# A two-layer graph network on one core: subtracting the segment maxima on TensorE, and scanning in place in PSUM

## The chip, the cores and the metric

One core of one Trainium2 chip runs the whole program in one launch. Its engines are TensorE (PE, with its weight loads shown as PEld), VectorE (DVE), ScalarE (ACT), GpSimd (POOL) and SyncE (SP, which issues DMAs here). The metric is the device time of one execution in microseconds (us), as the median over several runs.

## The reference

6250 nodes of 128 features, 106,250 edges sorted by target node. Both layers gather a row of the source node for each edge, form a softmax over the edges that enter a node, and add up weighted rows per node:

```python
h = relu(layernorm(x))
# layer 0, softmax per feature
msg   = h[src] + edge_attr                      # [E, 128]
s     = msg * beta
m     = segment_max(s, dst)
e     = exp(s - m[dst])
denom = segment_sum(e, dst)
agg   = segment_sum(msg * (e / denom[dst]), dst)
x     = x + (agg @ H + bias + h)                # H from phm_rule and W
# layer 1: graph attention with 4 heads, one maximum per head, then elu
```

Only layer 0's `s - m[dst]` is touched by the change.

## The kernel before, in words

The edges are worked off in 208 groups (`NG`) of 512 (`GE`), each as four blocks of 128 edges on the partitions. Each engine has its own instruction stream, written as a software pipeline: `sweep_edges` runs a list of (lag, stage) pairs, so that in step s an engine does stage X of group s minus X's lag, in the order of the list. Semaphores tie the engines together. Nothing reorders the work: what is written first on an engine runs first.

Layer 0, for a group g, in the order of its data:

- SyncE loads the 512 edge rows into `msg` (ring of 8 groups), lists and flags for four groups at a time.
- GpSimd gathers the rows `h[src]` into `ring_h` with four indirect DMAs, 128 rows each (line 573, ring of 4 groups: `gather0(g)` waits for the lift of group g-4).
- ScalarE lifts `ring_h` into PSUM (`row_psum`, line 693), VectorE adds it to `msg` (`add0`, line 938).
- TensorE turns the messages, so that features lie on partitions and edges run along the columns, with four products by `beta_ident` (beta times the identity) into `bank[g % 2]` (`turn0`, line 1165).
- VectorE finds the segment maxima with two scans along the edges. A flag of minus 2^126 at each segment's start resets the running maximum. The first scan (line 917) runs forward over the turned messages into `run_max`; the second (line 920) runs backward over `run_max` and spreads each segment's maximum over its columns, into `seg_max`. A [128 x 1] instruction (line 927) computes by how much the maximum of a segment that is cut by the group's border has risen.
- VectorE subtracts: `diff` = turned messages minus `seg_max` (line 948). TensorE turns it back into `bank[2]` with four transposes (`unturn0`, line 1174).
- ScalarE exponentiates twice, into `wgt` (line 678, for the denominators) and into PSUM (line 681); VectorE multiplies the latter with `msg` (`products0`, line 955).
- TensorE adds up per node with one-hot matrices, eight f32 products of 128 columns (line 1156); ScalarE merges the sums into the accumulators in SBUF (lines 656 to 664).

The order of the stages in one step, with their lags: VectorE `add0` (0), `one_hot0` (0), `products0` (3), `maxima0` (1); TensorE `sums0` (4), `turn0` (0), `unturn0` (2); ScalarE `merge0` (5), `lift0` (0), `weigh0` (3); GpSimd `gather0` alone. A f32 product of 128 columns shows as two passes in the trace, a transpose as one.

Layer 1 uses the same `segment_max` on four partitions, one per head. There the first scan already writes to PSUM (`head_run`), and the second reads it from there.

Of the kernel before, what the change touches and what calls it, by code (L numbers as in the profile page):

```python
# [22 lines left out]
ALU = mybir.AluOpType  # L23
ACT = mybir.ActivationFunctionType

P = 128
# [33 lines left out]
def apart(eng):  # L60


    eng.nop(nofuse=True)


def later(item, n):

    return not isinstance(item, int) or item >= n


def gnn_kernel(nc, x_in, src_in, dst_in, ea_in, rule_in, w0_in, bias_in, beta_in, w1_in, a_in, out):
    N, D = x_in.shape
# [5 lines left out]
    GB = 4  # L78
    GE = GB * P
# [23 lines left out]
    with ctx:  # L103
        def sb(name, shape, dt=F32):
            return ctx.enter_context(nc.sbuf_tensor(name, shape, dt))
# [14 lines left out]
        ident = sb("ident", [P, P])  # L120
        beta_ident = sb("beta_ident", [P, P])
# [3 lines left out]
        head_mask = sb("head_mask", [P, H])  # L125
        head_spread = sb("head_spread", [H, D])
        head_pick = sb("head_pick", [P, H])
        junk = sb("junk", [1, 1])
        zero_row = sb("zero_row", [1, WIN], BF16)
        beta = sb("beta", [P, 1])  # L130
# [50 lines left out]
        msg = sb("msg", [P, RING, GB, TW])  # L181
        meta_g = sb("meta_g", [P, RING, 2 * GB], I32)
        flags = sb("flags", [P, 2, HALF * GE + 1], BF16)
        window = sb("window", [P, RING, GB, H])
        run_max = sb("run_max", [P, 2, GE])
        seg_max = sb("seg_max", [P, 2, GE])
        diff = sb("diff", [P, 2, GE])
        drop = sb("drop", [P, RING])
# [20 lines left out]
        head_run = sums[0:H, 1, 1, :]  # L209
        bank = [ctx.enter_context(nc.psum_tensor(f"bank{i}", [P, GE], F32)) for i in range(4)]  # L210
# [92 lines left out]
        L0, L1 = layer_sems(0), layer_sems(1)  # L303
# [468 lines left out]
        def _(dve):  # L772
# [74 lines left out]
            def h0(b, u, use):  # L847
                if u in DVE_SLOTS:
                    dve.wait_ge(ln0_numbers, b + 1)
                    if later(b, WXB):  # L850
                        dve.wait_ge(h_stored[u], 16 * use)
                    made = use * len(DVE_SLOTS) + DVE_SLOTS.index(u)
                    if later(b, 2):
                        dve.wait_ge(ln0_part, 3 * made)
                    apart(dve)
                    for t in range(GB):
                        ins = dve.tensor_scalar(run_max[:, 0, t * D:(t + 1) * D],
                                                nodes[:, bass.ds(b * GB + t, 1), :].rearrange("p a d -> p (a d)"),
                                                norm_b[:, u, 0, t:t + 1], norm_b[:, u, 1, t:t + 1], ALU.mult, ALU.add)
                    ins.then_inc(ln0_part, 1)  # L860
                    dve.wait_ge(ln0_part, 3 * made + 1)
                    lnx = run_max[:, 0, :].rearrange("p (t d) -> p t d", d=D)
                    dve.tensor_scalar(wgt[:, u, :, :], lnx, 0.0, None, ALU.max).then_inc(ln0_h[u], 1)
                    tiles = nodes[:, bass.ds(b * GB, GB), :]
                    dve.scalar_tensor_tensor(tiles, lnx, 0.0, tiles, ALU.max, ALU.add).then_inc(ln0_part, 2)

            sweep(dve, NBAT, WXB, [(0, h0)])


# [13 lines left out]
                    link(dve.tensor_tensor(phm[:, :, :], phm[:, :, :], phm_term[:, :, :], ALU.add))  # L883
            dve.sem_inc(phm_ready, 1)

            dve.tensor_scalar(beta_ident[:, :], ident[:, :], beta[:, 0:1], None, ALU.mult).then_inc(beta_ready, 1)

            for j in range(2):
                ins = dve.tensor_scalar(a_heads[:, j * H:(j + 1) * H], head_mask[:, :], a_col[:, j:j + 1], None, ALU.mult)
# [14 lines left out]

            def segment_max(g, s, use, k, n, data):
                par = s % 2
                run = run_max[0:n, par, :] if k is L0 else head_run
                run_end = run_max[0:n, 1 - par, GE - 1:GE] if k is L0 else seg_max[0:n, 1 - par, GE - 1:GE]
                lo = s % HALF * GE
                flag = flags[0:n, s // HALF, lo:lo + GE + 1]  # L910
                dve.wait_ge(k["flagged"][s // HALF], 16 * (use + 1))
                if isinstance(g, int) and g == 0:
                    before = -BIG
                else:
                    dve.wait_ge(k["dropped"], g)
                    before = run_end
                dve.tensor_tensor_scan(run, flag[:, 0:GE], data, before, ALU.add, ALU.max  # L917
                                       ).then_inc(k["scanned"], 1)
                dve.wait_ge(k["scanned"], 2 * g + 1)
                dve.tensor_tensor_scan(seg_max[0:n, par, ::-1], flag[:, GE:0:-1], run[:, ::-1], -BIG,  # L920
                                       ALU.add, ALU.max).then_inc(k["scanned"], 1)
                dve.wait_ge(k["scanned"], 2 * g + 2)
                if not (isinstance(g, int) and g == 0):
                    if later(g, RING):
                        dve.wait_ge(k["factored"], g - (RING - 1))

                    dve.scalar_tensor_tensor(drop[0:n, s:s + 1], run_end, seg_max[0:n, par, 0:1],
                                             flag[:, 0:1], ALU.subtract, ALU.add).then_inc(k["dropped"], 1)
                else:
                    dve.memset(drop[0:n, s:s + 1], 0.0).then_inc(k["dropped"], 1)  # L930
# [9 lines left out]
                                  ).then_inc(L0["added"], 1)  # L940

            def maxima0(g, s, use):
                par = s % 2
                dve.wait_ge(L0["msgT"], g + 1)
                segment_max(g, s, use, L0, P, bank[par][:, :])
                if later(g, 2):
                    dve.wait_ge(L0["unturned"], g - 1)
                dve.tensor_tensor(diff[:, par, :], bank[par][:, :], seg_max[:, par, :], ALU.subtract
                                  ).then_inc(L0["shifted"], 1)

            def products0(g, s, use):
                if later(g, 2):
# [102 lines left out]
            def maxima1(g, s, use):  # L1055
                dve.wait_ge(L1["msgT"], g + 1)
                segment_max(g, s, use, L1, H, bank[1][0:H, :])
# [60 lines left out]
        def _(pe):  # L1118
# [20 lines left out]
            for par in range(1):  # L1139
                for j in range(2):  # L1140
                    ins = pe.matmul(sums[:, par, j, :], zero_row[0:1, 0:P], zero_row[0:1, :], start=True, stop=True)
# [18 lines left out]
            def turn0(g, s, use):  # L1160
                pe.wait_ge(L0["added"], g + 1)
                if later(g, 2):
                    pe.wait_ge(L0["shifted"], g - 1)
                for b in range(GB):
                    ins = pe.matmul(bank[s % 2][:, b * P:(b + 1) * P], msg[:, s, b, 0:D], beta_ident[:, :],  # L1165
                                    start=True, stop=True)
                ins.then_inc(L0["msgT"], 1)

            def unturn0(g, s, use):
                pe.wait_ge(L0["shifted"], g + 1)  # L1170
                if later(g, 1):
                    pe.wait_ge(L0["weighed"], g)
                for b in range(GB):
                    ins = pe.transpose(bank[2][:, b * P:(b + 1) * P], diff[:, s % 2, b * P:(b + 1) * P], ident[:, :])
                ins.then_inc(L0["unturned"], 1)

            def sums0(g, s, use):
# [134 lines left out]
```

## Time and profile before

| | |
|---|---|
| median of three runs | 2367.47 us (2364.91 to 2371.19) |
| the profiled execution | 2366.12 us, span 2364.4 us |
| TensorE busy | 1784.6 us (75%) |
| VectorE busy | 2110.9 us (89%) |
| ScalarE busy | 1390.4 us (59%) |
| GpSimd busy | 1641.5 us (69%) |
| gathers of layer 0, first and last start | 67.8 and 1130.3 us |
| gathers of layer 1, first and last start | 1251.5 and 2294.7 us |

How to read it: the span is what the profiler saw between the first and the last instruction of one execution; the execution's own time is 1.7 us more, and lies 1.4 us under the median. Layer 0's edges take the time from about 68 to 1155 us, layer 1's from about 1251 to 2330. Busy shares are averages over both layers and the parts between them, so what bounds one layer has to be read inside it. An engine's "issue" idle time is time in which it waited for nothing that the profile shows.

### The profile page before, as it was taken

The page shows a single profiled execution, that of the slowest core. Times are in us where ns is not written, and L with a number is a line of the kernel's source. Part 1 is how long each engine was busy: PE and PEld are TensorE (multiplying, and loading weights), DVE is VectorE, ACT ScalarE, POOL GpSimd, SP SyncE. Part 2 cuts the span into 40 slices and gives each one's busy share as a digit, 9 for nine tenths or more (in the row PEclk, how much of TensorE's full clock was granted, in tenths as well). Part 3 has the DMA queues.
Part 4 walks back from the last instruction along what each step waited for, and adds up shares of the span by engine and source line. Part 5 has one row for each costly group of instructions (what it writes and reads, how often), then busy time and mean ns, then how long its engine had stood idle before and what let it go on. Part 6 is the DMA issues. An engine that isn't in the chain of part 4 may idle for free.

```text
span 2364.4 us, 61321 instructions
## 1 busy us (share of the span) xinstructions
PE 1784.6 (75%) x14154; PEld 1649.2 (70%) x14155; DVE 2110.9 (89%) x4087; ACT 1390.4 (59%) x3516; POOL 1641.5 (69%) x1735
## 2 busy tenths in 40 slices
PE   0466666666666666666557999999999999999986
PEld 0366666666666666666457888888888888888886
DVE  5799999999999999999666898888888888988885
ACT  2366666666666666666783555555555555555554
POOL 3677777777777777777216777777777777777761
PEclk9999999999999999999767999999999999999995
DMA  5544444444444444444013333333333333333321
GB/s 126 144 129 133 128 131 129 126 128 127 132 128 132 128 132 130 126 126 122 9 33 74 61 59 59 59 59 59 59 59 59 59 59 59 59 59 59 59 52 55
DMA packets 338883, 214.19 MB, mean 91 GB/s; under 512 B 170833, under 2 KB 305340, under 8 KB 338829
## 3 DMA queue, kind: packets, MB, share of 16 engines
q0 software_dynamic: 53248, 112.57, 20.1%
q1 hardware_dynamic: 285580, 101.01, 16.8%
q8 instruction: 22, 0.36, 0.1%
q14 instruction: 33, 0.26, 0.0%
HBM read 201.38 MB, written 10.30 MB: 90 GB/s over the span
## 4 chain that ended last, share of the span: by engine, by line
POOL 56%; issue 24%; DMA 7%; DVE 6%; PE 2%; ACT 2%; SPq 1%; POOLq 1%; DVEq 0%; ACTq 0%
POOL ring_h L573 28%; POOL msg L595 28%; DMA ring_h<-h_dram,meta_g 4%; DMA msg<-wx_dram,meta_g 2%; DVE sums L917 1%; DVE seg_max L920 1%; PE sums L1156 1%; DVE onehot L901 1%; DVE prod L1071 1%; POOL diff L584 1%; ACT sums L693 1%; ACT acc L664 0%; PE bank L1281 0%; PE bank L1224 0%; SPq L331 0%
## 5 line engine op out<-in xcount | busy, mean ns | idle before, releaser
L595 POOL DMA_INDIRECT msg<-wx_dram,meta_g x832 | 790.8, 950 | 293.5 <-issue 247.0
L573 POOL DMA_INDIRECT ring_h<-h_dram,meta_g x832 | 810.2, 974 | 259.9 <-issue 257.8
L1156 PE MATMUL sums<-onehot,prod 128*128 128x128 f32 x3328 | 696.2, 293 | 28.7 <-ACT acc L664 14.6
L1156 PE MATMUL sums<-onehot,wgt 128*128 128x128 f32 x3328 | 676.3, 287 | 0.0
L1156 PEld LDWEIGHTS sums<-onehot,prod 128*128 128x128 f32 x3328 | 536.7, 203 | 74.6 <-issue 71.6
L1156 PEld LDWEIGHTS sums<-onehot,wgt 128*128 128x128 f32 x3328 | 538.3, 204 | 0.0
L1165 PE MATMUL bank<-beta_ident,msg 128*128 128x128 f32 x1664 | 243.5, 290 | 347.3 <-DVE msg L938 347.3
L1165 PEld LDWEIGHTS bank<-beta_ident,msg 128*128 128x128 f32 x1664 | 203.8, 193 | 387.7 <-DVE msg L938 336.7
L664 ACT ACTIVATE acc<-sums 128x1022 f32 x414 | 424.1, 1024 | 0.1
L693 ACT ACTIVATE sums<-ring_h 128x512 f32<-128x512 f32 x208 | 125.2, 602 | 385.2 <-DMA ring_h<-h_dram,meta_g 385.2
L917 DVE TENSOR_TENSOR_SCAN sums<-flags,seg_max,bank 4x512 f32<-4x512 bf16 x207 | 264.1, 1276 | 5.2 <-PE bank L1254 3.6
L917 DVE TENSOR_TENSOR_SCAN run_max<-flags,run_max,bank 128x512 f32<-128x512 bf16 x207 | 263.4, 1272 | 0.0
L920 DVE TENSOR_TENSOR_SCAN seg_max<-flags,run_max 128x512 f32<-128x512 bf16 x208 | 254.7, 1224 | 7.1
L920 DVE TENSOR_TENSOR_SCAN seg_max<-flags,sums 4x512 f32<-4x512 bf16 x208 | 251.1, 1207 | 7.1
L656 ACT ACTIVATE carried<-acc,scale 128x2 f32 x414 | 120.9, 292 | 184.1 <-PE sums L1156 163.8
L1245 PEld LDWEIGHTS bank<-window,onehotT 128*128 128x128 f32 x1664 | 210.8, 198 | 3.4 <-ACT onehotT L741 2.9
L1245 PE MATMUL bank<-window,onehotT 128*128 128x4 f32 x1664 | 205.1, 247 | 2.3 <-DMA window<-wx_dram 1.5
L729 ACT ACTIVATE sums<-logit_d 128x16 f32<-128x16 f32 x208 | 39.1, 188 | 267.0 <-DVE logit_d L1063 263.2
L901 DVE TENSOR_SCALAR onehot<-iota_f,meta_g 128x128 f32<-128x128 f32 x832 | 181.2, 276 | 5.9 <-DMA meta_g<-meta 5.8
L938 DVE TENSOR_TENSOR msg<-msg,sums 128x512 f32<-128x512 f32 x208 | 141.0, 678 | 13.8 <-ACT sums L693 13.5
L1071 DVE TENSOR_TENSOR prod<-sums,msg 128x512 f32<-128x512 f32 x208 | 140.1, 673 | 4.3 <-PE sums L1156 4.2
L955 DVE TENSOR_TENSOR prod<-sums,msg 128x512 f32<-128x512 f32 x208 | 141.9, 682 | 1.9 <-ACT sums L681 1.9
(159 smaller groups left out, 2706.0 us busy)
## 6 DMA issues: line engine op xcount, KB each, us to landing
msg<-in_edge_attr SPq DMA_DIRECT2D x207, 256.0 KB, 3.1
flags<-flag_dram SPq DMA_DIRECT2D x52, 512.2 KB, 4.0
ring_h<-h_dram,meta_g POOLq DMA_INDIRECT x832
msg<-wx_dram,meta_g POOLq DMA_INDIRECT x832
window<-wx_dram SPq DMA_DIRECT2D x832, 2.0 KB
wx_dram<-msg SPq DMA_DIRECT2D x13, 272.0 KB, 2.4
nodes<-in_x SPq DMA_DIRECT2D x4, 768.0 KB, 8.2
h_dram<-wgt SPq DMA_DIRECT2D x12, 256.0 KB, 2.4
```

Of the source, the lines that this page charges most:

```text
L573: pool.indirect_dma_start(hg[:, s % HRING, b, :], None, h_dram, bass.IndirectOffsetOnAxis(ap=meta_g[:, s, b:b + 1], axis=0)).then_inc(L0[" ...
L595: pool.indirect_dma_start(msg[:, s, b, :], None, wx_dram, bass.IndirectOffsetOnAxis(ap=meta_g[:, s, b:b + 1], axis=0)).then_inc(L1["gather ...
L664: act.activation(acc[:, :, bass.ds(node + 1, WIN - 1)], sums[:, par, :, 1:WIN], ACT.Copy).then_inc(k["merged"], 1)
L693: act.activation(row_psum, ring_h[:, s % HRING, :], ACT.Copy).then_inc(L0["lifted"], 1)
L901: ins = dve.tensor_scalar(onehot[:, s, b, :], iota_f[:, :], key[:, b:b + 1], None, ALU.is_equal)
L917: dve.tensor_tensor_scan(run, flag[:, 0:GE], data, before, ALU.add, ALU.max).then_inc(k["scanned"], 1)
L920: dve.tensor_tensor_scan(seg_max[0:n, par, ::-1], flag[:, GE:0:-1], run[:, ::-1], -BIG, ALU.add, ALU.max).then_inc(k["scanned"], 1)
L955: dve.tensor_tensor(prod[:, s % 2, :, :], wgt_psum.rearrange("p (b d) -> p b d", b=GB), msg[:, s, :, 0:D], ALU.mult).then_inc(L0["multipli ...
L1071: dve.tensor_tensor(prod[:, s % 2, :, :].rearrange("p b (h d) -> p b h d", h=H), head, msg[:, s, :, 0:D].rearrange("p b (h d) -> p b h d", ...
L1156: ins = pe.matmul(sums[:, 0, j, bass.ds(off, P)], what[:, slot, b, :], onehot[:, s, b, :], start=(b == 0), stop=(b == GB - 1), skip_group_ ...
L1165: ins = pe.matmul(bank[s % 2][:, b * P:(b + 1) * P], msg[:, s, b, 0:D], beta_ident[:, :], start=True, stop=True)
L1245: ins = pe.matmul(bank[2][:, b * H:(b + 1) * H], onehotT[:, s % 2, b * P:(b + 1) * P], window[:, s, b, :], start=True, stop=True)
```

## The change

Layer 0 no longer subtracts on VectorE. The first scan writes its running maxima over the turned messages, in the same PSUM bank, and the second scan reads them there. The turned messages are then gone, so TensorE builds the difference anew, in the layout with edges on partitions, as a sum of products that accumulate in `bank[2]`: beta times the messages, one product of 512 columns with `beta_ident` as weights, and minus the turned-back maxima, four products of `seg_max` with `neg_ident`, minus the identity. `neg_ident` is made once in the setup by VectorE. `run_max` goes; the setup uses `diff` as scratch in its place. Layer 0's `run_end`, the running maximum at the end of the group before, is now read from the last column of `seg_max`, as in layer 1. The waits move along: the turn of group g waits for the second scan of group g-2 where it waited for its subtraction; the second scan waits until TensorE has read the `seg_max` of two groups before, which the subtraction did for `diff`; the four products wait for the second scan.

```diff
+            dve.tensor_scalar(neg_ident[:, :], ident[:, :], -1.0, None, ALU.mult)
...
             def segment_max(g, s, use, k, n, data):
                 par = s % 2
-                run = run_max[0:n, par, :] if k is L0 else head_run
-                run_end = run_max[0:n, 1 - par, GE - 1:GE] if k is L0 else seg_max[0:n, 1 - par, GE - 1:GE]
+                run = data if k is L0 else head_run
+                run_end = seg_max[0:n, 1 - par, GE - 1:GE]
...
                 dve.wait_ge(k["scanned"], 2 * g + 1)
+                if k is L0 and later(g, 2):
+                    dve.wait_ge(L0["unturned"], g - 1)
                 dve.tensor_tensor_scan(seg_max[0:n, par, ::-1], flag[:, GE:0:-1], run[:, ::-1], -BIG,
                                        ALU.add, ALU.max).then_inc(k["scanned"], 1)
...
             def maxima0(g, s, use):
-                par = s % 2
                 dve.wait_ge(L0["msgT"], g + 1)
-                segment_max(g, s, use, L0, P, bank[par][:, :])
-                if later(g, 2):
-                    dve.wait_ge(L0["unturned"], g - 1)
-                dve.tensor_tensor(diff[:, par, :], bank[par][:, :], seg_max[:, par, :], ALU.subtract
-                                  ).then_inc(L0["shifted"], 1)
+                segment_max(g, s, use, L0, P, bank[s % 2][:, :])
...
             def turn0(g, s, use):
                 pe.wait_ge(L0["added"], g + 1)
                 if later(g, 2):
-                    pe.wait_ge(L0["shifted"], g - 1)
+                    pe.wait_ge(L0["scanned"], 2 * g - 2)
...
             def unturn0(g, s, use):
-                pe.wait_ge(L0["shifted"], g + 1)
                 if later(g, 1):
                     pe.wait_ge(L0["weighed"], g)
+                pe.matmul(bank[2][:, :].rearrange("p (b d) -> p b d", b=GB), beta_ident[:, :], msg[:, s, :, 0:D],
+                          start=True, stop=False, skip_group_check=True)
+                pe.wait_ge(L0["scanned"], 2 * g + 2)
                 for b in range(GB):
-                    ins = pe.transpose(bank[2][:, b * P:(b + 1) * P], diff[:, s % 2, b * P:(b + 1) * P], ident[:, :])
+                    ins = pe.matmul(bank[2][:, b * P:(b + 1) * P], seg_max[:, s % 2, b * P:(b + 1) * P], neg_ident[:, :],
+                                    start=False, stop=(b == GB - 1), skip_group_check=True)
                 ins.then_inc(L0["unturned"], 1)
```

VectorE, one step inside layer 0's loop, before (a scan is printed as SCALAR_TENSOR_TENSOR, out<-in; a name in brackets is a semaphore, its last digit 0 the layer):

```order
L938 TENSOR_TENSOR msg<-msg,sums 128x4x128 [waits lifted0]
L964 TENSOR_TENSOR onehot<-bank,meta_g 128x512 [waits listed0_0,summed0]
L955 TENSOR_TENSOR prod<-sums,msg 128x512 [waits weighed0,summed0]
L917 SCALAR_TENSOR_TENSOR run_max<-flags,run_max,bank 128x512 [waits dropped0,flagged0_0,msgT0]
L920 SCALAR_TENSOR_TENSOR seg_max<-flags,run_max 128x512 [waits scanned0]
L927 SCALAR_TENSOR_TENSOR drop<-run_max,seg_max,flags 128x1 [waits factored0,scanned0]
L948 TENSOR_TENSOR diff<-bank,seg_max 128x512 [waits unturned0]
```

and the same step in the changed kernel:

```order
L941 TENSOR_TENSOR msg<-msg,sums 128x4x128 [waits lifted0]
L962 TENSOR_TENSOR onehot<-bank,meta_g 128x512 [waits listed0_0,summed0]
L953 TENSOR_TENSOR prod<-sums,msg 128x512 [waits weighed0,summed0]
L918 SCALAR_TENSOR_TENSOR bank<-flags,seg_max,bank 128x512 [waits dropped0,flagged0_0,msgT0]
L923 SCALAR_TENSOR_TENSOR seg_max<-flags,bank 128x512 [waits unturned0,scanned0]
L930 SCALAR_TENSOR_TENSOR drop<-seg_max,flags 128x1 [waits factored0,scanned0]
```

The subtraction is gone, its wait for `unturned0` stands before the second scan, and that scan reads `bank` (PSUM) where it read `run_max` (SBUF).

TensorE, from the turn to the first sums of one step inside the loop, before:

```order
L1165 MATMUL bank<-beta_ident,msg 128x128 [waits shifted0,added0]
L1165 MATMUL bank<-beta_ident,msg 128x128 x3
L1174 MATMUL bank<-ident,diff 128x128 [waits weighed0,shifted0]
L1174 MATMUL bank<-ident,diff 128x128 x3
L1156 MATMUL sums<-onehot,prod 128x128 [waits merged0,multiplied0,onehots0]
```

and in the changed kernel:

```order
L1163 MATMUL bank<-beta_ident,msg 128x128 [waits scanned0,added0]
L1163 MATMUL bank<-beta_ident,msg 128x128 x3
L1170 MATMUL bank<-msg,beta_ident 128x512 [waits weighed0]
L1174 MATMUL bank<-neg_ident,seg_max 128x128 [waits scanned0]
L1174 MATMUL bank<-neg_ident,seg_max 128x128 x3
L1154 MATMUL sums<-onehot,prod 128x128 [waits merged0,multiplied0,onehots0]
```

The four transposes have become a product of 512 columns and four of 128; the sums stand behind them as before.

## Rows read from the trace of the kernel before

**Rows 1.** The page's part 4, the chain that ended last, by line.
```profile
POOL ring_h L573 28%; POOL msg L595 28%; DMA ring_h<-h_dram,meta_g 4%; DMA msg<-wx_dram,meta_g 2%; DVE sums L917 1%; DVE seg_max L920 1%; PE sums L1156 1%; DVE onehot L901 1%; DVE prod L1071 1%; POOL diff L584 1%; ACT sums L693 1%; ACT acc L664 0%; PE bank L1281 0%; PE bank L1224 0%; SPq L331 0%
```

**Rows 2.** Gathers: group | busy, mean ns | idle before; line 573 alone: min/median/max ns.
```profile
L573 POOL DMA_INDIRECT ring_h<-h_dram,meta_g x832 | 810.2, 974 | 259.9 <-issue 257.8 <-ACT sums L693 2.1
L595 POOL DMA_INDIRECT msg<-wx_dram,meta_g x832 | 790.8, 950 | 293.5 <-issue 247.0 <-DMA meta_g<-meta 40.2 <-DVE prod L1071 6.4
...
L573 POOL DMA_INDIRECT ring_h<-h_dram,meta_g x832: 940/944/1572, 67.8 to 1130.3; - x167
```

**Rows 3.** Timeline, layer 0, VectorE and GpSimd: start us, duration us, instruction [idle before].
```profile
705.84 0.68 DVE L938 TENSOR_TENSOR msg<-msg,sums 128x512 f32<-128x512 f32 x1
...
707.63 1.27 DVE L917 TENSOR_TENSOR_SCAN run_max<-flags,run_max,bank 128x512 f32<-128x512 bf16 x1
...
708.62 0.94 POOL L573 DMA_INDIRECT ring_h<-h_dram,meta_g  x1 [0.30 <-issue]
...
708.94 1.22 DVE L920 TENSOR_TENSOR_SCAN seg_max<-flags,run_max 128x512 f32<-128x512 bf16 x1
...
709.86 1.05 POOL L573 DMA_INDIRECT ring_h<-h_dram,meta_g  x1 [0.30 <-issue]
710.20 0.22 DVE L927 SCALAR_TENSOR_TENSOR drop<-run_max,seg_max,flags 128x1 f32<-128x1 f32 x1
...
710.33 0.69 DVE L948 TENSOR_TENSOR diff<-bank,seg_max 128x512 f32<-128x512 f32 x1
...
710.93 0.68 DVE L938 TENSOR_TENSOR msg<-msg,sums 128x512 f32<-128x512 f32 x1
```

**Rows 4.** Timeline, layer 0: a scan and gather near the start; first, last long gather.
```profile
87.81 1.23 DVE L920 TENSOR_TENSOR_SCAN seg_max<-flags,run_max 128x512 f32<-128x512 bf16 x1
...
88.22 1.57 POOL L573 DMA_INDIRECT ring_h<-h_dram,meta_g  x1 [0.30 <-issue]
...
127.20 1.05 POOL L573 DMA_INDIRECT ring_h<-h_dram,meta_g  x1 [0.30 <-issue]
...
1128.96 1.03 POOL L573 DMA_INDIRECT ring_h<-h_dram,meta_g  x1 [0.31 <-issue]
```

**Rows 5.** Timeline, layer 1: a second scan and a gather inside it.
```profile
1500.88 1.21 DVE L920 TENSOR_TENSOR_SCAN seg_max<-flags,sums 4x512 f32<-4x512 bf16 x1
1501.45 0.94 POOL L595 DMA_INDIRECT msg<-wx_dram,meta_g  x1 [0.30 <-issue]
```

**Rows 6.** VectorE's groups by form: layer 1's second scan, and an in-place instruction.
```profile
L920 DVE TENSOR_TENSOR_SCAN seg_max<-flags,sums 4x512 f32<-4x512 bf16 x208 | 251.1, 1207 | 7.1
...
L996 DVE SCALAR_TENSOR_TENSOR bank<-diff,bank 128x512 f32<-128x512 f32 x12 | 8.4, 696 | 28.7 <-POOL diff L584 28.7
```

**Rows 7.** Stretches: PE, PEld, DVE, ACT, POOL busy, PEclk; ScalarE's waits, 115 to 1100 us.
```profile
115.00:600.00 485.00, 328.37 (x2657) 304.75 (x2656) 477.19 (x665) 307.70 (x760) 369.29 (x380) 1.00 0.46 130
1300.00:2340.00 1040.00, 946.80 (x7713) 879.75 (x7712) 908.89 (x2212) 595.40 (x1634) 758.58 (x802) 0.93 0.30 57
...
ACT sums L693 <- DMA ring_h<-h_dram,meta_g: 334.1, 188, 3.8
```

**Rows 8.** Timeline of TensorE, one step of layer 0.
```profile
706.57 1.16 PE L1165 MATMUL bank<-beta_ident,msg 128*128 128x128 f32 x8 [1.33 <-DVE msg L938]
707.56 0.60 PE L1174 MATMUL bank<-ident,diff 128*128 128x128 f32 x4
708.00 0.39 PE L1156 MATMUL sums<-onehot,prod 128*128 128x128 f32 x2
...
709.56 0.39 PE L1156 MATMUL sums<-onehot,wgt 128*128 128x128 f32 x2
```

**Rows 9.** Timeline, end of layer 0: ScalarE's last lift and last merge.
```profile
1134.15 0.60 ACT L693 ACTIVATE sums<-ring_h 128x512 f32<-128x512 f32 x1 [3.11 <-DMA ring_h<-h_dram,meta_g]
...
1153.68 1.02 ACT L664 ACTIVATE acc<-sums 128x1022 f32 x1
```

## What was predicted before the run

> **What bounds the kernel now.** I read the chain of waits first. It puts layer 0's time on GpSimd's indirect gathers and on the "issue" time between them, and next to nothing on VectorE [rows 1]. The groups by line say the same from the other side: before the gathers of line 573 GpSimd has only issue time, and 2.1 us in all for anything it waited for [rows 2]. So in layer 0 GpSimd never stops from its first gather (67.8 us) to its last (1130.3 us) [rows 2], and what decides is how long one gather takes.
>
> VectorE looks like the bound too: busy 477 of 485 us in the stretch from 115 us, [rows 7]. Yet ScalarE's lift, which hands the gathered rows to VectorE's add, waits for the gather's landing 188 times, 334 us [rows 7], so the landing is late for ScalarE and still in time for VectorE. Two independent engines that are both never idle for a thousand microseconds have to be tied together. The tie is in the gathers' durations. One gather normally takes 0.94 us, and the next starts 0.30 us after its end, so a group of four needs 4 x (0.944 + 0.304) = 4.99 us. VectorE's cycle is 5.09 to 5.10 us (add at 705.84, add at 710.93) [rows 3]. In each cycle one gather takes 1.03 to 1.05 us in place of 0.94 [rows 3], which brings GpSimd to VectorE's cycle. I went through all 832 gathers. From 125 us on there are 197 long ones, one per group (the first and the last of them are in [rows 4]). Each started while the second scan (line 920, flags and `run_max`, both in SBUF) was running and ended 0.75 us after that scan's end (10th to 90th percentile 0.749 to 0.754): at 709.86 + 1.05 = 710.91 against a scan that ended at 708.94 + 1.22 = 710.16 [rows 3]; at the start, before the two cycles have locked, at 88.22 + 1.57 = 89.79 against 87.81 + 1.23 = 89.04 [rows 4]. A gather that starts inside the first scan, whose data come from PSUM, takes 0.94 us, always (708.62 in [rows 3]). So does one that starts inside layer 1's second scan, which reads flags from SBUF and its data from PSUM: 1501.45, 0.94 us, inside the scan of 1500.88 [rows 5]; there are 205 such and none is long. So the second scan with two SBUF inputs holds GpSimd's gather until it ends, and that couples GpSimd to VectorE.
>
> **The change part by part.** (1) *The subtraction leaves VectorE.* 208 instructions of 0.69 us; of each, 0.60 us counts in the cycle (710.33 to 710.93, the next add) [rows 3]. VectorE's cycle falls from 5.09 to 4.49 us. On the engine that is 208 x 0.60 = 125 us. Almost none of it reaches the end: GpSimd needs 4.99 us a group, and from there VectorE waits 0.5 us in each group for the lift.
>
> (2) *The second scan reads its data from PSUM.* Its form becomes that of layer 1's: 1.207 us on average against 1.22 [rows 3, 6], so no price of its own. It now has one SBUF input, and by the 205 cases of layer 1 it holds no gather. All long gathers of layer 0 lose their excess: 810.2 us busy against 832 x 0.944 = 785.4 us, **-24.8 us**, on the path, since GpSimd never waits. This is the term that I count. The Trainium skill, SBUF — State Buffer, section "Who interferes with whom", says that a VectorE instruction with two SBUF inputs contends with a GpSimd instruction that reads SBUF; this trace agrees, with 197 of 197. The same section also infers that such an instruction does not stall descriptor generation, which would need the write interface; by that the excess would have another cause and would stay (the second rival below). The trace speaks against it.
>
> (3) *The first scan writes over its input in PSUM.* Not shown for a scan. The lower bound is nothing. For an upper one, the only instruction that works in place on a PSUM bank, line 996, takes 0.696 us for 512 columns, where the subtraction takes 0.69 [rows 3, 6]: 0.01 us. Even 0.4 us more would leave VectorE under 4.99. I take 0.
>
> (4) *TensorE takes over the subtraction.* Per group it runs now: turn 0.99 us (706.57 to 707.56), four transposes 0.44 (to 708.00), sixteen passes of the sums 1.56 + 0.22 = 1.78 [rows 8]; 3.21 us of 5.10. The four transposes become one 512-column product and four 128-column ones of two passes. The latter cost 0.89 us, as eight passes do in the sums. The 512-column product in f32 stands nowhere in the trace. From below it is one pair of passes, 0.22 us; from above four times that, 0.89 us; I take 0.89, since it moves four times the columns. Sum 0.99 + 0.89 + 0.89 + 1.78 = 4.55 us (3.9 with the lower bound), so TensorE is full to nine tenths but under 4.99. Its granted clock is 1.00 in layer 0, and in layer 1, where it is busier, 0.93 [rows 7]; at 0.93 the 4.55 become 4.9, still under.
>
> (5) *Waits.* The turn waits for the second scan of two groups before (once: the subtraction); VectorE has run that before the add on which the turn waits anyway. The second scan waits for the maxima of two groups before to be read by TensorE. Behind it on VectorE stand the drop and the next group's add, on which turn and all else hang, but that product is issued right behind the turn of the previous group and ends about 3.4 us after that group's add begins; the scan comes 3.1 us into the next cycle, so 4.7 us later. The 512-column product waits for the second exponential of the group before, which ends about 1.0 us after the add begins and is needed at 1.65. ScalarE's merge for the next sums ends about 2.7 us after the add begins, needed at 3.4. All are covered, by 0.6 us or more.
>
> (6) *The end of layer 0.* From the last gather (1130.3 [rows 2]) to the last merge (1153.68 + 1.02) it runs through landing, lift (1134.15), and then sums and merges in turn [rows 9]. TensorE's extra 1.3 us stand once ahead of the first of these sums: +0.6 us by the order of work. If the last landing takes 1.6 us, as most do, and not 2.9 as here, -1.3. I take +0.3. (7) `neg_ident` costs 0.28 us ahead of a VectorE wait of 9 us for the first lift: nothing.
>
> **Sum.** -24.8 + 0.3 = -24.5 us on the profiled execution's 2366.1 us (span 2364.4), so 2341.6. The median of the runs is 1.4 us above that execution: **2343 us**.
>
> **The rivals.** *The gathers stay long.* If what holds the gather is not the second SBUF input but something that also the new scan has (reading flags, writing `seg_max`), GpSimd is held as before wherever the two meet; at one meeting per group and the same 0.12 us, layer 0 stays at its cycle and the time at 2366 to 2368 us. For it: in layer 1 gathers are also a little longer than 0.944 on average, 0.950 [rows 2], which I put down to the one-hot of line 901. Against it: 205 gathers inside the scan with the new form, none long. In part (the drop, three small SBUF operands, 0.22 us, catching some gathers) it gives 2350 to 2360 us.
>
> *TensorE becomes the bound, and the kernel slower.* The place is the 512-column product with its wait, in front of the four that accumulate on it. From 4.99 - 3.66 = 1.33 us for it on, TensorE sets the cycle; from 1.45 us on the kernel is slower than before. If f32 streams in it at twice the time per column of the rows (1.79 us), the cycle is 5.45 us and layer 0 costs 208 x 0.35 = 73 us more: 2440 us. A drain of 0.7 us a group between its parts gives 5.25 us and +30, 2397 us. For it: TensorE has only 0.44 us to spare by my sum, and the products now stand in one queue behind three waits. Against it: passes of 128 columns follow each other every 0.11 us also across the border between two kinds of product (707.56 and 708.00) [rows 8].
>
> **How the numbers follow.** The forecast case gets 0.81, its own range 2336 to 2349; the partly held gathers 0.07 (2350 to 2360), fully held 0.06 (2366), TensorE 0.06 (2370 and up). Leaving out the last two and a little of the first, the range is 2336 to 2354. A measurement of this kernel can't tell less than about 0.3%, 7 us, from no change. So faster 0.88, same 0.07, slower 0.05.
>
> **What the profile after would show.** Right: the gathers of line 573 busy 785 to 788 us at a mean of 944 to 948 ns; first gather at 68, last at about 1105; VectorE's add waiting for the lift in most groups, some 90 us in all; VectorE busy some 130 us less in sum; TensorE's cycle with gaps of 0.3 to 0.5 us; layer 1 unchanged. Wrong: gathers with a mean near 974; or GpSimd waiting for lifts (then TensorE or ScalarE is late); or a TensorE without gaps in layer 0; or a scan over 1.6 us.

## The result, and the profile after

| | before | changed |
|---|---|---|
| first comparison, median | 2369.33 us (2364.91 to 2373.57, 4 runs) | 2347.94 us (2346.46 to 2351.67, 4 runs) |
| ratio, 95% interval | | 0.9912 (0.9889 to 0.9936) |
| repeated, five runs | 2367.09 us | 2341.48 us, ratio 0.9894 (0.9880 to 0.9907) |
| a third time, another chip | 2367.22 us | 2342.90 us, ratio 0.9902 (0.9878 to 0.9925) |
| the profiled execution | 2366.12 us, span 2364.4 | 2351.67 us, span 2348.8 |
| VectorE busy | 2110.9 us | 2001.9 us |
| TensorE busy | 1784.6 us | 2036.4 us |

The kernel is 0.9 to 1.1% faster, some 21 to 26 us; 2343 was forecast. The profiled execution of the first comparison is the slowest of its four, so it is only 14.5 us faster than the profiled one before. The medians are of all executions, the ratios of the fast ones alone: in the third comparison one of the changed kernel's four executions took 4403.69 us, and two of the seven before took 2403 and 2410 us.

The gathers, from the groups by line of the profile after, against [rows 2]; the columns are busy us, mean ns, and idle before with what ended it:

```profile
L595 POOL DMA_INDIRECT msg<-wx_dram,meta_g x832 | 793.2, 953 | 293.5 <-issue 246.5
L573 POOL DMA_INDIRECT ring_h<-h_dram,meta_g x832 | 787.3, 946 | 260.1 <-issue 253.7
```

Layer 0's gathers take 787.3 us where they took 810.2. Of the 203 that were over 0.985 us, one is left, the first. Minimum, median and maximum in ns, first and last start in us:

```profile
L573 POOL DMA_INDIRECT ring_h<-h_dram,meta_g x832: 943/947/1142, 67.7 to 1107.5; - x167
```

In the repetition:

```profile
L595 POOL DMA_INDIRECT msg<-wx_dram,meta_g x832 | 790.7, 950 | 292.9 <-issue 246.9 <-DMA meta_g<-meta 39.5 <-DVE prod L1069 6.4
L573 POOL DMA_INDIRECT ring_h<-h_dram,meta_g x832 | 785.3, 944 | 259.9 <-issue 257.2 <-ACT sums L693 2.1 <-DMA meta_g<-meta 0.6
```

There the mean is the undisturbed 944 ns; in the first profile every gather, of layer 1 too, is some 3 ns longer. The idle time before the gathers is as before, 260 us, with 5.5 us of it put down to lifts. So GpSimd still hardly stops, and it now runs at its own pace.

The other side is VectorE. One step from the timeline after (start us, duration us), against [rows 3] and [rows 5]:

```profile
704.32 1.22 DVE L923 TENSOR_TENSOR_SCAN seg_max<-flags,bank 128x512 f32<-128x512 bf16 x1
...
704.66 0.94 POOL L573 DMA_INDIRECT ring_h<-h_dram,meta_g  x1 [0.30 <-issue]
...
705.58 0.22 DVE L930 SCALAR_TENSOR_TENSOR drop<-seg_max,flags 128x1 f32<-128x1 f32 x1
...
705.73 0.69 DVE L941 TENSOR_TENSOR msg<-msg,sums 128x512 f32<-128x512 f32 x1
```

A gather that starts inside the second scan now takes 0.94 us; 204 do, and the longest takes 0.957. VectorE's add waits for the lift 89.7 us in all (about 90 was predicted), and the groups by form show what the new scans cost:

```profile
L918 DVE TENSOR_TENSOR_SCAN bank<-flags,seg_max,bank 128x512 f32<-128x512 bf16 x207 | 264.8, 1279 | 0.0
L923 DVE TENSOR_TENSOR_SCAN seg_max<-flags,bank 128x512 f32<-128x512 bf16 x208 | 253.9, 1221 | 7.2
L941 DVE TENSOR_TENSOR msg<-msg,sums 128x512 f32<-128x512 f32 x208 | 143.0, 688 | 98.7 <-ACT sums L693 89.7
```

TensorE's step from the timeline after, against [rows 8]:

```profile
702.03 1.15 PE L1163 MATMUL bank<-beta_ident,msg 128*128 128x128 f32 x8 [1.10 <-DVE msg L941]
...
703.02 1.02 PE L1170 MATMUL bank<-msg,beta_ident 128*128 128x512 f32 x2
...
703.88 1.05 PE L1174 MATMUL bank<-neg_ident,seg_max 128*128 128x128 f32 x8
...
704.77 0.39 PE L1154 MATMUL sums<-onehot,prod 128*128 128x128 f32 x2
...
706.56 1.15 PE L1163 MATMUL bank<-beta_ident,msg 128*128 128x128 f32 x8
```

From one turn to the next without a wait it takes 4.53 us: turn 0.99, the 512-column product 0.86, the four products 0.89, the sums 1.79.

The two spans are 15.6 us apart. In parts: the last gather of layer 0 ends at 1108.4 us in place of 1131.2 (-22.8). From there to the last merge it takes 26.0 in place of 23.5 us (+2.5). Layer 1's gathers take 1046.7 in place of 1044.1 us (+2.6), what follows them 70.9 in place of 68.7 us (+2.2), and the part between the layers is 0.1 us shorter. The parts of layer 1 and behind it are not touched by the change, and in the repetition they are 1044.0 and 66.3 us: they vary from one execution to the next. The +2.5 at the end of layer 0 can be read from the trace. The last lift starts 3.1 us after the last gather's end, where it was 2.9 before and is 2.7 in the repetition. TensorE waited 1.87 us for it, and its granted clock then fell from 1.00 to 0.50 (2.4 to 1.2 GHz) from 1113.1 to 1116.6 us:

```profile
1111.50 0.60 ACT L693 ACTIVATE sums<-ring_h 128x512 f32<-128x512 f32 x1 [3.25 <-DMA ring_h<-h_dram,meta_g]
...
1112.88 1.87 PE L1163 MATMUL bank<-beta_ident,msg 128*128 128x128 f32 x8 [1.87 <-DVE msg L941]
...
1114.54 1.91 PE L1170 MATMUL bank<-msg,beta_ident 128*128 128x512 f32 x2
```

The turn takes 1.87 and the product 1.91 us there, against 1.15 and 1.02 above. The clock fell once more at 1130.2 us, and the last of layer 0's sums ran at 0.50. In the repetition this end takes 22.9 us, and the clock stays at 1.00 through it.

### The profile page after: what moved, and what is told of

The parts are those of the page before. It is cut to its first block, busy times and chain, and to the rows that moved or that the text cites. A ratio compares the mean times of both kernels' runs of the same rounds, so it can differ in the third digit from the quotient of the medians.

```text
span 2348.8 us, 63839 instructions
## 1 busy us (share of the span) xinstructions
PE 2036.4 (87%) x15402; PEld 1824.6 (78%) x15403; DVE 2001.9 (85%) x3880; ACT 1397.5 (59%) x3516; POOL 1621.2 (69%) x1735
## 4 chain that ended last, share of the span: by engine, by line
POOL 44%; issue 22%; DMA 14%; DVE 9%; PE 6%; ACT 4%; SPq 1%; POOLq 0%; DVEq 0%; ACTq 0%
POOL msg L595 24%; POOL ring_h L573 19%; DMA ring_h<-h_dram,meta_g 10%; DMA msg<-wx_dram,meta_g 3%; PE sums L1154 2%; DVE sums L918 2%; DVE seg_max L923 2%; ACT sums L693 2%; DVE onehot L902 1%; DVE prod L1069 1%; ACT acc L664 1%; POOL diff L584 1%; PE bank L1163 0%; PE bank L1282 0%; SPq L471 0%
## 5 line engine op out<-in xcount | busy, mean ns | idle before, releaser
L573 POOL DMA_INDIRECT ring_h<-h_dram,meta_g x832 | 787.3, 946 | 260.1 <-issue 253.7
L1174 PEld LDWEIGHTS bank<-neg_ident,seg_max 128*128 128x128 f32 x1664 | 219.0, 192 | 100.5 <-issue 100.0
L918 DVE TENSOR_TENSOR_SCAN bank<-flags,seg_max,bank 128x512 f32<-128x512 bf16 x207 | 264.8, 1279 | 0.0
L923 DVE TENSOR_TENSOR_SCAN seg_max<-flags,bank 128x512 f32<-128x512 bf16 x208 | 253.9, 1221 | 7.2
L941 DVE TENSOR_TENSOR msg<-msg,sums 128x512 f32<-128x512 f32 x208 | 143.0, 688 | 98.7 <-ACT sums L693 89.7
L1174 PE MATMUL bank<-neg_ident,seg_max 128*128 128x128 f32 x1664 | 219.5, 275 | 0.0
L1170 PE MATMUL bank<-msg,beta_ident 128*128 128x512 f32 x416 | 214.7, 598 | 0.0
```

The costliest lines, as they stand in the source:

```text
L573: pool.indirect_dma_start(hg[:, s % HRING, b, :], None, h_dram, bass.IndirectOffsetOnAxis(ap=meta_g[:, s, b:b + 1], axis=0)).then_inc(L0[" ...
L941: dve.tensor_tensor(msg[:, s, :, 0:D], msg[:, s, :, 0:D], row_psum.rearrange("p (b d) -> p b d", b=GB), ALU.add).then_inc(L0["added"], 1)
L1170: pe.matmul(bank[2][:, :].rearrange("p (b d) -> p b d", b=GB), beta_ident[:, :], msg[:, s, :, 0:D], start=True, stop=False, skip_group_che ...
L1174: ins = pe.matmul(bank[2][:, b * P:(b + 1) * P], seg_max[:, s % 2, b * P:(b + 1) * P], neg_ident[:, :], start=False, stop=(b == GB - 1), s ...
```

## The experiments

The theory is the prediction's: the second scan, while it reads two operands from SBUF, holds a gather until it ends, and that ties GpSimd to VectorE's cycle; the time of the change comes from its end. The rival: VectorE's shorter cycle is what counts, and the long gathers are a by-product of a busy VectorE. Four runs move the two halves of the change apart; the others ask about TensorE's margin and about layer 1.

**changed_again**: the changed kernel, no edit.

> The changed kernel once more, as the yardstick for the others on this chip. Expected 0.991 of the time before, 2346 to 2350 us, gathers of layer 0 busy 785 to 789 us with at most a few over 0.985 us.

Measured: 2341.48 us, ratio 0.9894 (0.9880 to 0.9907), one gather over 0.985 us. This is 4.5 us under the expected times, with a ratio just under the expected one.

**scan_only**: one half of the change on the kernel before.

```diff
-                run = run_max[0:n, par, :] if k is L0 else head_run
-                run_end = run_max[0:n, 1 - par, GE - 1:GE] if k is L0 else seg_max[0:n, 1 - par, GE - 1:GE]
+                run = data if k is L0 else head_run
+                run_end = seg_max[0:n, 1 - par, GE - 1:GE]
```

> The kernel before, with its first scan in place in PSUM and its second reading from there, and the subtraction still on VectorE (its result is the running maxima minus the segment maxima, not the messages minus them, so the outputs are not the reference's). Theory (the second scan holds a gather through its second SBUF input): the long gathers are gone, 785 to 789 us busy, a mean of 944 to 948 ns. But VectorE's cycle is still 5.09 us, so GpSimd runs ahead by 0.1 us a group until the ring of four stops it: time 2362 to 2370 us, ratio 0.998 to 1.001. Rival (the gathers are lengthened by any scan of this length, or by VectorE being always busy): 190 or more gathers over 0.985 us, 808 to 812 us busy, same time.

Measured: 2363.92 us, ratio 0.9986 (0.9977 to 0.9995). In its timeline VectorE is as busy as before, the subtraction stands where it stood, and a gather starts inside the scan:

```profile
1004.44 1.22 DVE L920 TENSOR_TENSOR_SCAN seg_max<-flags,bank 128x512 f32<-128x512 bf16 x1
...
1004.75 0.94 POOL L573 DMA_INDIRECT ring_h<-h_dram,meta_g  x1 [0.30 <-issue]
1005.70 0.22 DVE L927 SCALAR_TENSOR_TENSOR drop<-seg_max,flags 128x1 f32<-128x1 f32 x1
1005.83 0.68 DVE L948 TENSOR_TENSOR diff<-bank,seg_max 128x512 f32<-128x512 f32 x1
```

One gather is over 0.985 us, and they are 785.1 us busy:

```profile
L573 POOL DMA_INDIRECT ring_h<-h_dram,meta_g x832 | 785.1, 944 | 271.2 <-issue 250.2 <-ACT sums L693 11.3 <-DMA meta_g<-meta 9.8
```

That is the theory, and the rival of this run falls: where the second scan's data lie decides about the holds, not VectorE's load. GpSimd runs ahead and is stopped in another place, as its waits from 60 to 1120 us show (total us, times, longest us; the longest of "issue" is the one before the first gather):

```profile
POOL ring_h L573 <- issue: 250.2, 787, 6.6
POOL ring_h L573 <- ACT sums L693: 11.3, 37, 0.3
POOL ring_h L573 <- DMA meta_g<-meta: 9.8, 8, 1.4
```

Before, it waited 2.1 us in all; now it waits 9.8 us for lists, which are loaded only when VectorE has done the one-hots of the half ring before, and 11.3 us are put down to lifts. VectorE's cycle of 5.09 us sets the end. Of the 3 us that are nevertheless gained some 1.8 stand in the traces: before 125 us, while the cycles were not locked yet, five gathers were held in the kernel before, and VectorE's add waits 11.7 us for lifts in place of 13.5. The rest is open.

**subtract_only**: the other half. The changed kernel with the scans through SBUF again.

```diff
+        run_max = sb("run_max", [P, 2, GE])
...
-                run = data if k is L0 else head_run
+                run = run_max[0:n, par, :] if k is L0 else head_run
```

> The changed kernel with run_max back in SBUF: the first scan writes it there, the second reads it there, TensorE does the subtraction. Theory (held gathers): VectorE's cycle is 4.49 us and follows GpSimd, so where the scan meets the gathers is set by the landing time, and a gather can be held for any part of 1.22 us. With the landings of the trace (1.6 to 2.9 us) the scan covers the first gather of the next group in about every second group: 0.2 to 0.6 us a group, 40 to 120 us more than the changed kernel, 2385 to 2470 us. At the least 150 gathers are over 0.985 us. Rival (what matters is only that VectorE has 0.6 us less to do, the hold is a by-product of its 5.09 us cycle): the time of the changed kernel, 2345 to 2352 us.

Measured: 2477.43 us (2469.05 to 2482.02), ratio 1.0461 (1.0441 to 1.0482). Its timeline:

```profile
703.60 1.22 DVE L924 TENSOR_TENSOR_SCAN seg_max<-flags,run_max 128x512 f32<-128x512 bf16 x1
703.87 1.71 POOL L574 DMA_INDIRECT ring_h<-h_dram,meta_g  x1 [0.30 <-issue]
704.95 0.22 DVE L931 SCALAR_TENSOR_TENSOR drop<-seg_max,flags 128x1 f32<-128x1 f32 x1
705.88 0.94 POOL L574 DMA_INDIRECT ring_h<-h_dram,meta_g  x1 [0.30 <-issue]
706.25 0.69 DVE L942 TENSOR_TENSOR msg<-msg,sums 128x512 f32<-128x512 f32 x1 [1.08 <-ACT sums L694]
...
709.35 1.23 DVE L924 TENSOR_TENSOR_SCAN seg_max<-flags,run_max 128x512 f32<-128x512 bf16 x1
709.63 1.71 POOL L574 DMA_INDIRECT ring_h<-h_dram,meta_g  x1 [0.30 <-issue]
```

The groups by line:

```profile
L574 POOL DMA_INDIRECT ring_h<-h_dram,meta_g x832 | 917.8, 1103 | 259.9 <-issue 257.8 <-ACT sums L694 1.8 <-DMA meta_g<-meta 0.3
L942 DVE TENSOR_TENSOR msg<-msg,sums 128x512 f32<-128x512 f32 x208 | 143.1, 688 | 225.6 <-ACT sums L694 223.8 <-issue 1.7
```

With 0.6 us less to do on VectorE the kernel is 110 us slower than before. The gather of 703.87 takes 1.71 us and ends at 705.58, 0.76 us after the scan's end at 704.82: the relation of [rows 3], now with a hold of 0.77 us in place of 0.10. The gathers' 917.8 us against 785.3 are 132.5 us, and the spans of this kernel and of changed_again differ by 139.6. The theory had the direction and the mechanism and put the size too low, 2385 to 2470 us: it had a hold in about every second group, 0.2 to 0.6 us a group on average. In the trace 172 of the 208 groups have one, of 0.79 us in the median (10th to 90th percentile 0.57 to 0.92), and VectorE's cycle is 5.8 us in the median. The trace suggests who leads as the reason; no run moves the scan alone. Before, VectorE's 5.09 us were the longer cycle, so GpSimd slid back until a gather met only the last part of the scan (0.92 us after its start in [rows 3]) and lost only the difference of the two cycles. Here VectorE waits for GpSimd (the add, 223.8 us), so the landing sets when the scan comes, and the held gather begins early in it, 0.24 us after its start in the median.

**dead_subtraction**: the changed kernel, with the subtraction kept on VectorE as dead work.

```diff
                 segment_max(g, s, use, L0, P, bank[s % 2][:, :])
+                dve.tensor_tensor(diff[:, s % 2, :], bank[s % 2][:, :], seg_max[:, s % 2, :], ALU.subtract
+                                  ).then_inc(L0["shifted"], 1)
...
-                    pe.wait_ge(L0["scanned"], 2 * g - 2)
+                    pe.wait_ge(L0["shifted"], g - 1)
```

> The changed kernel, with a subtraction of the old size added on VectorE whose result nobody reads but for the turn's wait, so VectorE's cycle is 5.09 us again. Theory: GpSimd is free (gathers 785 to 789 us busy), but VectorE sets the cycle: 2366 to 2373 us, ratio 0.998 to 1.003. TensorE has 0.5 us to spare. Rival (VectorE's load does not matter once the gathers are free): 2346 to 2352 us.

Measured: 2364.75 us, ratio 0.9995 (0.9985 to 1.0004); the gathers 785.2 us busy:

```profile
L573 POOL DMA_INDIRECT ring_h<-h_dram,meta_g x832 | 785.2, 944 | 270.4 <-issue 251.6 <-ACT sums L693 11.0 <-DMA meta_g<-meta 7.8
```

The free gathers alone bring nothing as long as VectorE needs 5.09 us. The four combinations are now all measured: the scan in PSUM alone gives 3 us, the subtraction on TensorE alone costs 110 us, and both together give 25.

**product_1_5x, product_2x** and their repetitions: a 256-column or a second 512-column product ahead of the first, on the changed kernel. The edit of product_2x; that of product_1_5x has `bank[2][:, 0:GE // 2]` and half of `msg` in the new product:

```diff
+                pe.matmul(bank[2][:, :].rearrange("p (b d) -> p b d", b=GB), beta_ident[:, :], msg[:, s, :, 0:D],
+                          start=True, stop=False, skip_group_check=True)
                 pe.matmul(bank[2][:, :].rearrange("p (b d) -> p b d", b=GB), beta_ident[:, :], msg[:, s, :, 0:D],
```

> The changed kernel with a 256-column product added in front of the 512-column one (it is overwritten). The trace has the 512-column product at 0.86 us, so TensorE's work per group goes from 4.53 to 4.96 us, just under GpSimd's 4.99. Theory (TensorE has 0.46 us to spare): the time of the changed kernel or up to 10 us more, 2341 to 2352 us. Rival (TensorE is on the path already through its latency, as ScalarE and VectorE wait behind it): 0.43 us a group, 80 us or more, 2420 us and up.

> The changed kernel with the 512-column product done twice. TensorE's work per group 5.39 us, over GpSimd's 4.99. Theory: TensorE sets the cycle of layer 0, 208 x 0.4 = 83 us more than the changed kernel, 2415 to 2435 us, and GpSimd waits for the lifts. Rival (some of the product hides behind the load of weights or in gaps): under 2380 us.

> The kernel of product_1_5x again, for the same reason. TensorE's work per group 4.96 us. Theory (TensorE has 0.46 us to spare): 2341 to 2352 us. Rival (TensorE is on the path through its latency): 0.43 us a group, 2420 us and up.

> The kernel of product_2x again, as in the first call ScalarE stood still for up to 8 us at a time in every kernel, the one before included (3289 us). The changed kernel with the 512-column product done twice. TensorE's work per group 5.39 us, over GpSimd's 4.99. Theory: TensorE sets the cycle of layer 0, 208 x 0.4 = 83 us more than the changed kernel, 2415 to 2435 us. Rival (some of the product hides): under 2380 us.

Measured: 3463.53 and 3474.65 us, repeated 3453.49 and 3466.17, while the kernel before took 3288.81 and 3292.49 us beside them (ratios 1.0521, 1.0557, 1.0475 and 1.0529). In these series, on chips 13 and 14, engines stood still at a releaser that the profile calls "remote". ScalarE did so for 985 to 1036 us in each of the four traces, in layer 0's loop for up to 8 us at a time and once for 23 us; in layer 1 VectorE did too (222 us ahead of line 1046 in product_1_5x). Six minutes earlier chip 13 had run the kernel before in 2367.09 us, so the standstills are not tied to a chip's number. In product_2x_again, from 200 to 1600 us:

```profile
POOL ring_h L573 <- ACT sums L693: 482.9, 106, 6.1
ACT wgt L678 <- remote: 415.3, 62, 8.4
```

"remote" is a releaser that the profile doesn't see. What bounds the kernel then is not what bounds it otherwise: the kernels with 1.5 and with 2 products are 11 and 13 us apart, where 208 x 0.43 = 89 us of product lie between them. These times say nothing on TensorE's margin, and it stays open. One thing can be read from a step of product_2x that had no gap:

```profile
806.44 1.02 PE L1170 MATMUL bank<-msg,beta_ident 128*128 128x512 f32 x2
807.30 1.02 PE L1172 MATMUL bank<-msg,beta_ident 128*128 128x512 f32 x2
808.16 1.05 PE L1176 MATMUL bank<-neg_ident,seg_max 128*128 128x128 f32 x8
```

The product costs 0.86 us each time, so the second would put TensorE at 5.39 us a group, over the gathers' 4.99, if nothing else were in the way.

**layer1_psum_iota** (three times): the same idea in layer 1. Its four one-hot instructions of a group read and write SBUF alone; here one instruction reads the column numbers from PSUM, and layer 1 scans in place too, which frees the bank for them.

```diff
-        head_run = sums[0:H, 1, 1, :]
+        iota_psum1 = sums[:, 1, 1, 0:P]
...
-                key = meta_g[:, s, GB:2 * GB].bitcast(F32)
-                for b in range(GB):
-                    ins = dve.tensor_scalar(onehot[:, s, b, :], iota_f[:, :], key[:, b:b + 1], None, ALU.is_equal)
-                ins.then_inc(k["onehots"], 1)
+                key = meta_g[:, s, GB:2 * GB].bitcast(F32).rearrange("p (b a) -> p b a", a=1).to_broadcast([P, GB, P])
+                steps = iota_psum1.rearrange("p (a n) -> p a n", a=1).to_broadcast([P, GB, P])
+                dve.tensor_tensor(onehot[:, s, :, :], steps, key, ALU.is_equal).then_inc(k["onehots"], 1)
...
-                run = data if k is L0 else head_run
+                run = data
...
+            dve.wait_ge(mid_wx, NBAT)
+            link(dve.tensor_copy(iota_psum1, iota_f[:, :]))
...
-                    pe.wait_ge(L1["scanned"], 2 * g - 1)
+                    pe.wait_ge(L1["scanned"], 2 * g)
```

> The changed kernel, with layer 1 treated alike: its one-hots are made by one instruction that reads the column numbers from PSUM (in the bank that the running maxima leave free, as layer 1's first scan now works in place too), in place of four that read and write SBUF only. Theory (an instruction on VectorE holds a gather when it uses the second SBUF port): the 60 to 85 long gathers of layer 1 go, 791 to 785 us busy, 5 to 8 us less: 2333 to 2338 us. Against it: TensorE turns layer 1's logits only after both scans of the group before, 1.2 us later. Rival (that wait decides): 2345 to 2400 us.

> The kernel of layer1_psum_iota again, for the same reason. Its first trace has no long gather in layer 1 (787 us busy). Theory: 5 to 8 us less than the changed kernel, 2333 to 2338 us. Rival (the turn's later wait decides, and its first ratio, 1.034 with all else slow, points there): 2345 to 2450 us, with GpSimd waiting for layer 1's products.

> The kernel of layer1_psum_iota a third time: in its first two calls ScalarE stood still for up to 8 us at a time in every kernel, the one before included. Where that is over: theory, 5 to 8 us less than the changed kernel, ratio to before 0.986 to 0.989, no long gather in layer 1. Rival (the later turn decides): ratio 0.990 to 1.03, GpSimd waiting in layer 1.

Measured: 3393.51, 3404.11 and 3451.12 us, ratios 1.0342, 1.0346 and 1.0319 to the kernel before, all with the same standstills. The time is not settled. The holds are. Minimum, median and maximum of layer 1's gathers, in layer1_psum_iota_third and then in product_1_5x, which has layer 1 as it was and ran under the same condition:

```profile
L595 POOL DMA_INDIRECT msg<-wx_dram,meta_g x832: 942/947/983, 1799.4 to 3371.2; - x167
```

```profile
L595 POOL DMA_INDIRECT msg<-wx_dram,meta_g x832: 938/944/1097, 1782.3 to 3399.1; - x167
```

No gather of layer 1 is over 0.985 us in any of the three, where product_1_5x has 71. So the one-hots held them, as the prediction said of line 901. Whether the later turn of layer 1 costs more than these 5 to 8 us can't be told from here: the gathers of layer 1 take 1573 to 1578 us from first to last in these three traces, and 1574 to 1618 in the four product traces, whose layer 1 is the old one.

**changed_stalled**: the changed kernel again, meant for the condition of those series.

> The changed kernel on chips in the state of the last three calls, where ScalarE stands still for up to 8 us at a time and the kernel before takes 3290 to 3340 us. There GpSimd waits for ScalarE's lifts in layer 0, so a freed gather is worth nothing, and TensorE's 1.3 us more per group stand in the ring of turn, exponential, products and sums behind each stall. Theory: slower than before, ratio 1.03 to 1.05 (layer 0 as in layer1_psum_iota, 1532 to 1580 us between first and last gather, layer 1 as in product_1_5x, 1618 us). Rival (the kernels of those calls are slower only by what was added to them): ratio 0.98 to 1.00.

Measured: it came on chip 11, where nothing stood still, 2342.90 us against 2367.22, ratio 0.9902 (0.9878 to 0.9925), the gathers of layer 0 785.3 us busy. It is a third comparison of the change. Whether the change costs time where the engines stand still is open: the changed kernel as it is was never measured there.

## Why the prediction was right

- *The long gathers, -24.8 us, the term on which it rested.* Measured -22.9 us in the first profile (787.3 against 810.2) and -24.9 in the two others (785.3). The last gather of layer 0 began at 1107.5, 1105.3 and 1105.4 us; "about 1105" was predicted. That the hold hangs on the second scan's data in SBUF is shown by scan_only (the data in PSUM, VectorE as busy as before: the long gathers vanish) and by subtract_only (the data in SBUF again: they come back and grow).
- *The gathers stay long, at 0.06 and in part at 0.07.* Neither came. The part put down to the drop can be looked up: in the five traces whose second scan reads PSUM and that ran undisturbed, 125 gathers of layer 0 begin inside the drop, which reads `seg_max` and `flags` from SBUF, and the longest takes 0.954 us. The prediction calls the first of its rivals "the second rival below" where it speaks of the Trainium skill.
- *The inference in the Trainium skill, SBUF — State Buffer, "Who interferes with whom", by which the excess would have stayed.* The Trainium skill infers there that a VectorE instruction with two SBUF inputs doesn't stall descriptor generation. For these gathers that didn't hold: in scan_only the excess went when the second SBUF input went. What the same section of the Trainium skill states on a GpSimd instruction that reads SBUF does hold for them, 197 of 197 before; they read their offsets from `meta_g` in SBUF. A DMA of GpSimd without offsets in SBUF was not run.
- *The subtraction's 0.60 us, of which almost nothing reaches the end.* VectorE's cycle without a wait is 4.53 us (701.20 to 705.73; 4.49 was predicted), and the add waits 89.7 us. But the prediction priced the two halves apart, as if the freed gathers gave the gain and VectorE's relief only went with it. The runs show that they give it together: in scan_only and dead_subtraction the gathers are as free as in the changed kernel, and the time stays within 3 us of the old one, because VectorE still needs 5.09 us a group. VectorE's busy time fell by 109.0 us, not by some 130; an estimate for 11 of the missing 21 us is that in 122 groups the add now waits, and the 0.09 us by which it overlapped the instruction ahead is gone.
- *The scans.* 1.279 and 1.221 us against 1.27 and 1.22: working in place or from PSUM costs 0.01 us at most.
- *TensorE.* 4.53 us against 4.55; the 512-column product, for which there was no row, 0.86 us, near the upper bound of 0.22 to 0.89. That 0.89 was the right end to take was not shown beforehand. The work stays under 4.99 us, and the granted clock in layer 0 remains 1.00 up to 1113 us. That TensorE would be the bound, and the kernel slower, did not happen; how close it is, no run could tell.
- *The end of layer 0, +0.3 us.* +2.5 in the first profile, -0.6 in the repetition (22.9 against 23.5 us): within the bounds of -1.3 and +0.6 except where the clock fell at the last turn, which I had not counted.
- *The sum.* -24.5 us was forecast, -21 to -26 measured in the three comparisons. Of the two profiled executions, on the first of which the forecast was built, the one after is only 14.5 us faster, by the parts that vary.

## What to carry to other kernels

When two engines are both never idle for long, look for what ties them: sort the durations of the "same" instruction and see whether the long ones end at a fixed distance after something on the other engine. Here two kinds of VectorE instructions held GpSimd's indirect gathers, and both had all their operands in SBUF: the scan over flags and data, and layer 1's one-hots. With one input in PSUM neither held any. The [128 x 1] drop of 0.22 us, with both inputs in SBUF, held none of 125, so look at the durations before you move an operand. And relieve both partners of such a pair: freeing the gathers alone gave 3 us, and relieving VectorE alone cost 110 us, because it changed where in the scan the two meet.

## What the runs showed of the hardware that was not expected

- The size of a hold differs with the same scan and the same gather: 0.10 us a group before, and 0.79 us in the median of the held ones in subtract_only. In both the held gather ends 0.75 to 0.76 us after the scan.
- Layer 1's held gathers end 0.82 us after an instruction of line 901 that was running when they began (63 gathers over 0.985 us before, 10th to 90th percentile 0.817 to 0.824).
- A f32 product of 128 columns and one of 4 columns both take 0.11 us a pass; one of 512 columns 0.43 us. No run shows why the first two agree.
- In three of the series, on chips 13 and 14, ScalarE and VectorE stand still at a "remote" releaser, ScalarE for 0.93 to 1.17 ms in a trace, and the kernel before takes 3289 to 3342 us in place of 2367. None of the seven undisturbed traces has one such wait. Chip 13 ran both ways within six minutes. The cause is open.
